# Adding the second sum's halves ahead of the low weight halves and block 2's one-hots

## The reference

```
xn   = layernorm(x)
agg  = segment_sum(xn[src], dst, 6250)
h    = relu(agg @ W_rel + b_rel + xn @ W_root)          # 256 -> 512
i, g, o = three gates of  h @ W_ih.T + b_ih + b_hh      # 512 -> 3 x 512
hl   = sigmoid(o) * tanh(sigmoid(i) * tanh(g))
x    = x + hl @ W_fc + b_fc                             # 512 -> 256
```

## Time and profile before

| | us |
|---|---|
| median of 3 runs (lowest, highest) | 1268.32 (1267.84, 1269.71) |
| the profiled execution, its own time | 1268.6 |
| its span, first to last instruction | 1266.8 |
| mean granted clock of TensorE | 0.985 |
| PE busy | 1120.1 (88%) |
| DVE busy | 836.6 (66%) |
| POOL busy | 805.2 (64%) |
| ACT busy | 624.0 (49%) |

### The profile page before, as it was taken

How to read it: one execution, slowest core, us unless ns; L and a number is a source line. 1 busy time by engine, 2 the same in 40 slices (tenths; PEclk the granted TensorE clock), 3 DMA queues, 4 the chain that set the end, 5 groups by cost and what they waited for, 6 DMA issues and landing times. The chain is left out here.

```text
span 1266.8 us, 26665 instructions
## 1 busy us (share of the span) xinstructions
PE 1120.1 (88%) x9821; PEld 975.9 (77%) x9821; DVE 836.6 (66%) x2587; ACT 624.0 (49%) x1250; POOL 805.2 (64%) x850
## 2 busy tenths in 40 slices
PE   1326889999899999999999999999998999999998
PEld 0315779787788887878788877888787888897798
DVE  7886466667467756776667656766675667646565
ACT  5672435555364545544554455444544554545332
POOL 5167777777777777777777777777777777500000
PEclk9997989999899999999999999999998999999999
DMA  9574435444444455444444454444444444323398
GB/s 326 190 250 116 121 112 146 144 139 116 142 145 137 113 146 146 136 124 138 145 137 135 123 146 139 136 124 145 145 129 121 145 137 137 97 68 98 116 346 292
DMA packets 89760, 188.47 MB, mean 149 GB/s; under 512 B 19195, under 2 KB 51937, under 8 KB 89647
## 3 DMA queue, kind: packets, MB, share of 16 engines
q0 software_dynamic: 39888, 108.97, 30.3%
q1 hardware_dynamic: 38900, 57.91, 13.9%
q10 hardware_dynamic: 10859, 20.05, 4.4%
HBM read 154.86 MB, written 32.00 MB: 148 GB/s over the span
## 5 line engine op out<-in xcount | busy, mean ns | idle before, releaser
L624 POOL DMA_INDIRECT ring<-table,sidx x813 | 782.0, 962 | 278.8 <-issue 278.8
L403 PE MATMUL ps<-h_h,wih_h 128*128 128x250 f32 x1200 | 340.8, 284 | 0.0
L404 PE MATMUL ps<-h_l,wih_h 128*128 128x250 f32 x1200 | 338.2, 282 | 0.0
L405 PE MATMUL ps<-h_h,wih_l 128*128 128x250 f32 x1200 | 338.1, 282 | 0.0
L403 PEld LDWEIGHTS ps<-h_h,wih_h 128*128 128x128 f32 x1200 | 232.1, 193 | 1.6 <-issue 0.4
L404 PEld LDWEIGHTS ps<-h_l,wih_h 128*128 128x128 f32 x1200 | 232.3, 194 | 1.1
L405 PEld LDWEIGHTS ps<-h_h,wih_l 128*128 128x128 f32 x1200 | 231.9, 193 | 0.0
L989 PE MATMUL ps<-ring,oneh 128*32 128x512 f16 x2321 | 149.1, 387 | 72.1 <-DMA ring<-table,sidx 47.2
L768 ACT ACTIVATE gate<-ps,bgate 128x250 f32<-128x250 f32 x300 | 124.4, 468 | 142.5 <-PE ps L405 142.5
L1426 DVE TENSOR_SCALAR oneh<-iota,didx 128x64 f16<-128x64 f16 (+2 forms) x1199 | 183.8, 258 | 0.9 <-issue 0.9
L989 PEld LDWEIGHTS ps<-ring,oneh 128*32 128x32 f16 x2321 | 61.8, 97 | 142.6 <-DMA ring<-table,sidx 61.7
(11 more groups left out here) (212 smaller groups left out, 2476.1 us busy)
## 6 DMA issues: line engine op xcount, KB each, us to landing
ring<-table,sidx POOLq DMA_INDIRECT x813
swt_d<-swt ACTq DMA_DIRECT2D x25, 500.0 KB
gate<-swt_d SPq DMA_DIRECT2D x19, 500.0 KB, 5.9
x_room<-in_x SPq DMA_DIRECT2D x12, 512.0 KB, 10.2
xn<-table SPq DMA_DIRECT2D x25, 224.0 KB
xin<-in_x SPq DMA_DIRECT2D x25, 224.0 KB
res<-xin SPq DMA_DIRECT2D x25, 224.0 KB
table<-tile_room SPq DMA_DIRECT2D x8, 512.0 KB, 2.7
```

The costliest lines, as they stand in the source:

```text
L403: eng.matmul(dst, wh, xh, start=first, stop=False)
L404: eng.matmul(dst, wh, xl, start=False, stop=False)
L405: return eng.matmul(dst, wl, xh, start=False, stop=last)
L624: pool.indirect_dma_start(ring[:, j, :], None, table, bass.IndirectOffsetOnAxis(ap=idx, axis=0)).then_inc(done, 16)
```

## The change

One call is moved by two lines in VectorE's turn 0: block 1's `add_halves` from behind `hots(2)` to directly behind block 0's.

```
@@ turn(), VectorE, t == 0
                     hots(0)
                     hots(1)
                     add_halves(0, 0)
+                    add_halves(0, 1)
                     low_w1()
                     hots(2)
-                    add_halves(0, 1)
                     return
```

## The result

The changed kernel takes 1270.79 us (median of 12 runs, 1268.69 to 1272.33), the kernel before 1267.92 on the same chip (12 runs, 1265.37 to 1270.14). The ratio is 1.0021 (95% interval 1.0012 to 1.003): about 2.7 us slower by the ratio, 2.9 between the medians. I had forecast no change, 1268.3, and a range up to 1270.5; both were wrong.

The account below looks back on a forecast made before the run. GpSimd's gather stream was taken as the bound. From 1268.6 us profiled: -0.05 to 0 at the adds, +3.3 graph layer, -3.3 waits for rows, 0 stream; the median, 0.3 lower, gives 1268.3 us, range 1266.2 to 1270.5.

Parts of the forecast that it names:

- What bounds the kernel: GpSimd's unbroken stream of gathers, about 1.25 us each, sets the end; TensorE, 88% busy, waits for it.
- The delay of the graph layer: On TensorE, the graph layer's first matmul starts 3.3 us later, near 107.0, released by VectorE's at_l.
- That this delay costs nothing: TensorE's shorter waits for rows absorb the 3.3 us by 162.33 at the latest; 0 us at the end.
- the 121.9 forecast: Sign in TensorE's profile: the cell gates' first matmul near 121.9, 2.1 us later than before.
- the lag: TensorE's lateness at the end of turn 1, 3.7 us at worst; reaching the end was a rival, 5%.
- The stream: GpSimd's gathers beside VectorE's moved work: neither held nor slowed, taken as 0 us, bounds -3.0 to +2.6.
- the stream is slowed: Rival: low_w1, low_wih and low_rest fall worse on GpSimd's gathers, same or slower; 12%, of which 2 slower.
- its outer bound: Slowed stream at most +2.6 us, giving 1270.9: three gathers beside low_w1 each losing as much as the worst.
- The port rule: VectorE's two-input instructions can block GpSimd's SBUF reads on shared ports; estimated +0.8 to +1.4 us net, not adopted.

Follow-up runs that it names:

- kernel with fills: Changed kernel with the eight subtractions of low_wih(0) and low_wih(1) replaced by zero fills of the same outputs that read nothing; ratio 1.0002 against the kernel before.
- one wait: Changed kernel with one wait more: before low_wih(0), VectorE waits until its own at_l is done; ratio 0.9996 against the kernel before.
- later run: Kernel before with block 3's 24 one-hots moved in turn 1 from behind low_rest to directly behind at_l, ahead of low_wih; ratio 1.0051.
- changed, again: Changed kernel run once more without an edit, for a second profile; ratio 1.0022 against the kernel before.
- 4 one-hots behind: Changed kernel with the last 4 of block 2's 25 one-hots behind low_wih(1) instead of ahead of at_l; ratio 1.0027 against the kernel before.
- 5 one-hots behind: Changed kernel with 5 of block 2's 25 one-hots behind low_wih(1) instead of ahead of at_l; ratio 1.0026 against the kernel before.
- low_w1 first: Changed kernel with low_w1 back at its old place, block 1's halves added behind it, then block 2's one-hots; ratio 1.0026 against the kernel before.
- one-hots between: Changed kernel with block 3's 24 one-hots spread three behind each subtraction of low_wih(0) and low_wih(1), not behind low_rest; ratio 1.0019 against the kernel before.
- one-hots first: Changed kernel with block 2's one-hots ahead of block 1's halves and low_w1 behind them; ratio 0.9996 against the kernel before.

## Why the prediction was wrong

- *What bounds the kernel*: right. The gathers are the clock of the kernel; no semaphore held one, and what one of them lost appears at the end.
- *The delay of the graph layer*: right, 3.05 us for 3.3, with the releaser named.
- *That this delay costs nothing*: right, and shown: the kernel with fills (106.38) and that with one wait (106.54) are as late and run at 1.0002 and 0.9996. The gates started at 123.44 instead of the 121.9 forecast, not through the lag but because block 2's rows came late.
- *The stream*: here the prediction failed, at the step "I take 0, since the nearest row, low_w1 at its old place, costs the same 0.46". I asked only what low_w1, the moved work, would cost gathers at its new place; that was near enough (1.32 us for one gather, 0.37 too much). I let low_wih and low_rest cost what they had cost before, since they kept their order and length. But the first eight of their subtractions lost the wait that had stood in front of them, and have block 2's one-hots there instead. Their three gathers of before had lost 0.5 us together (in its second profile they took 1.32, 1.10, 1.10); one gather now loses 3.85 - 0.95 = 2.90. The term was +2.4, less what other gathers happened to gain: all 813 together took 1.4 us more than in the first profile of before, and 2.7 more in the second profiles of both kernels.
- *The rivals*: "the stream is slowed" had the right place, GpSimd, and by its outer bound almost the right time (1270.9), but the wrong cause (low_w1 meeting three gathers as bad as the worst), and 12%; that the bound came near was luck. I also took the worst gather seen, 1.97 us, for the most that one can lose. It was the one at 117.37, which began in the very last subtraction and was held to its end: 117.30 + 1.22 + 0.82 = 119.34. Read so, it says that a gather is held to the end of the one subtraction that it met, and no row of the kernel before shows more; that one can wait through eight could not be read there. The range is also not what it says of itself: two thirds of +2.6 would be 1270.0, and it stops at 1270.5, still short of a bound that stood for another cause.
- *The port rule of the Trainium skill*, "SBUF — State Buffer", section "SBUF: two separate sides", that I weighed and set aside: its direction was right. The fills, which read nothing, lengthen no gather and the subtractions of two SBUF tensors do, which agrees with it. Its measure, one instruction, agrees with the gathers beside the run in the kernel before, and not with those of the table below: they were held through up to eight, and the measurement decides. The gather at 94.63, which I had counted against the rule, began with the last of low_w1's subtractions and got through first; that subtraction took 725 ns, the other three 682 or 683.

What stays open: what inside VectorE or GpSimd holds a gather through a series; whether the missing idle time is needed for it, the one-hots ahead, or both, since no kernel here has the run behind other unbroken work or behind one-hots of another form; and why later gathers lose more in one execution than in another, the some 2 us that the later run lost beside its two holds included. In the expectation for the one-wait kernel I named the overlap of neighbouring instructions (75 against 81 ns) as a mark of the two cases. It is not a clean one: in the second profile of the changed kernel a subtraction of the run lasts 548 ns (median) and overlaps the one before it by 79, in the first profile of before 548 and 80, and a gather is held in the one and not in the other.

## What to carry to other kernels

Where one engine's unbroken stream sets the time, ask of an edit not only what work it moves but which waits it takes away from other work: an idle moment of a busy engine can be what lets a neighbour through. Ask too what work then stands right ahead of what. A wait for one's own last result, about 0.1 us, in front of or within a series of two-input VectorE operations cost nothing here and spared the changed kernel its whole loss of some 3 us. And when the trace shows one bad sample, work out what it waited for before taking it for the worst case.

## What the runs showed of the hardware

A gather issued by GpSimd was held to the end of a series of back-to-back VectorE subtractions of two SBUF tensors, and ended 0.81 to 0.83 us behind the last of them, in nine cases:

| kernel | subtractions end | gather took | gather ends |
|---|---|---|---|
| changed | 110.40 | 3.85 | 111.22 |
| changed, again | 110.07 | 3.86 | 110.89 |
| run later | 110.35 | 4.37 | 111.17 |
| run later, low_wih(2) | 112.81 | 2.15 | 113.62 |
| 4 one-hots behind | 110.05 | 4.55 | 110.88 |
| 5 one-hots behind | 109.51 | 4.41 | 110.33 |
| low_w1 first | 108.17 | 4.14 | 108.98 |
| one-hots between, low_wih(2) | 116.93 | 1.88 | 117.75 |
| one-hots between, low_rest | 121.66 | 4.43 | 122.48 |

In all of these VectorE had come to the series without having waited right ahead of it, and had made one-hots since it last stood idle. Counted over all 14 profiles, 354 other lengthened gathers met an operation with two SBUF inputs and another such operation right behind it, with no one-hots since VectorE's last idle time, even one of 0.03 us: each of them ended 0.80 to 0.84 us behind the one operation that it had met. The runs show this as a pattern; that the one-hots cause it is not shown. With a wait there, of 2.60 us (before), 0.19 (one-hots first) or only for its own last result (one wait), and no one-hots behind the wait, the same subtractions lengthened a gather to between 0.99 and 1.32 us. Beside fills of the same size, and beside block 2's one-hots in the changed kernel, gathers took 0.95 us. Three one-hots or a short gap behind each subtraction let gathers through.
